# Count pieces of the second gathering layer moved ahead of its gathers, and two scatter tables filled from a small buffer, in a five-part graph network on one core

## The chip, the cores and the metric

The kernel runs on one core of one Trainium2 chip. The metric is device time of one execution in microseconds (us), lower is better. The kernel before was timed three times. The profile is of one execution more.

## The reference

Four graph layers follow one another on 6,250 nodes with 128 features, each ending in a residual sum and a layer norm. All share one list of 106,250 edges, sorted by target node.

```python
x = _layernorm(x + L0(x))   # segment_sum(weight * (x @ K)[dst], src) + bias
x = _layernorm(x + L1(x))   # sum over 8 bases b of segment_sum(alpha_b[type64] * (x[src] @ bases[b]), dst)
x = _layernorm(x + L2(x))   # relu(segment_sum(x[src] @ (W_data if type2 == 0 else W_control).T + b, dst) + x @ W_self.T + b_self)
x = _layernorm(x + L3(x))   # two graph convolutions with W1 and W2, normed by the degrees
```

Float32 results are kept by splitting a float32 table into three bf16 parts where a bf16 product is used.

## The kernel before, in words

The edges form 416 groups of 256, and 16 groups form a part (26 parts, each some 240 target nodes wide). The program is five passes, written out by hand for each engine as its own instruction stream. TensorE is `pe`, VectorE `dve`, ScalarE `act`, GpSimd `pool`, and `sp` only issues DMAs.

**Pass 0** (L0) is a scatter. In each of 52 bodies, four steps `k` make 4 tiles of 128 messages each. GpSimd adds them with indirect DMAs (L903) into four tables in device memory, `sums0` to `sums3`, in the fixed order 0, 1, 2, 3. A scatter into table `t` waits for the one before it into `t`. `sums0` starts as a copy of `x` (L883), `sums1` as the bias, written from a 2 KB buffer per partition (L884), `sums2` and `sums3` as zeros, written from the zeroed `acc`, 26 KB per partition (L892). The first zero fill waits until the product table `hx` is stored, the second until the first rows of `hx` are back (`xwin_in[0]`). `acc` is the upper part of `node_data`, where ScalarE also collects the adjacency counts of pass 0. So ScalarE waits for both fills before its first step. In the same pass TensorE counts edges per (source, target) pair (`build_adjacency`), ScalarE copies the counts to SBUF as integers (L1010) and stores them to `adj`.

**Pass 1** (L1) gathers rows of `t1` with indirect DMAs (L863, two per group, into a ring of 8 groups), multiplies them with weighted one-hots (`group_products`, L1325 and L1328), and once per part applies the eight bases (`base_piece`, L1416). Behind it run the stage steps of blocks of 256 nodes: TURN, RESIDUAL, NORM, TURN_ROWS, PROJECT (L1398, L1401), TABLE, then HI, REST, MID, LOW, which split the new rows into three bf16 parts and store them to `xp1` (L1150). The new table `t2` is stored by `sp` (L741, L744). There are 25 blocks (`NH`). The last two run after the last group, by themselves.

**Pass 2** (L2) covers the 26 parts in 13 pairs. Of each pair one part is gathered (32 indirect DMAs, L863, products at L1350), the other is computed from counts: seven pieces, each of 7 x 3 x 2 = 42 bf16 matmuls (`typed_piece`, L1506). A piece needs seven blocks of `x_parts`, the bf16 parts read back from `xp1` (L796), and two planes that ScalarE makes of a raw piece of counts (`to_planes`, L1166 and L1167, raw pieces loaded at L784). `typed_products` sets the order: two groups, one piece, and so on for eight steps, so that pieces stand in steps 0 to 6. Planes lie in `alpha`, the edge weights of pass 1. `x_parts` lies where pass 1 keeps its sums `G` and the last blocks' buffers.

**Passes 3 and 4** (L3) work alike with one plane per piece (L1447).

At the change from pass 1 to pass 2, `sp` waits until all of `xp1` and `t2` is stored and then loads all seven pieces of `x_parts`. TensorE waits for all seven before its first piece. ScalarE makes the first planes only when the last blocks are done. GpSimd starts gathering once `t2` is stored (`stored[1]`) and the first indices are copied (`idx_ready[2]`).

Of the kernel before, what the change touches and what calls it, by code (L numbers as in the profile page):

```python
# [41 lines left out]
P = 128  # L42
N = 6250
# [69 lines left out]
SET_FREE = (-3, 0, -1, 1, 2, 3, 5)  # L113
RAW2_USES = [RAW2.count(r) for r in range(3)]
# [42 lines left out]
def gnn_program(nc, src, src_row, dst, type2, type64, weight, x, xT0, k0, bias0, bases, rel_weights,  # L157
# [4 lines left out]
    with ctx:  # L162
# [351 lines left out]
        def sums_whole(eng, p, b):  # L514

            if p == 1:
                eng.wait_ge(based_added, NPT + 1 if isinstance(b, int) else b + (LAG + 1))
# [89 lines left out]
        def halves_in_steps(eng, stage_step, between=None):  # L607

            with eng.Fori(0, NH - 2) as b:
                if between:  # L610
                    between(b)
                for at in range(STEPS):
                    stage_step(b, 0, at)
            for at in range(STEPS):
                stage_step(NH - 2, 0, at)
                stage_step(NH - 1, 1, at)

# [8 lines left out]
        def parts_past(e):  # L626

            return {1: 0, 2: NH, 3: 2 * NH}[e]

# [42 lines left out]
        def _(sp):  # L672
# [91 lines left out]
            def reload_parts(layer, q):  # L764
# [7 lines left out]
                if q == NPC - 1:  # L772
                    sp.wait_ge(xp_in[NPC - 2], layer * 32 + 16)
# [3 lines left out]
            def load_typed(j, q):  # L777
                if q < 2:
                    sp.wait_ge(planes_ready, j * NPC + (q + 5))
                elif q < NPC - 1:  # L780
                    sp.wait_ge(planes_ready, j * NPC + (NPC + q - 1))
                else:
                    sp.wait_ge(planes_ready, j * NPC + NPC)
                sp.dma_start(raw2_in_words[RAW2[q]], adj[bass.ds(j * (2 * P) + 2 * P, P),  # L784
                                                         q * PIECE_H * CHUNK_COLS:(q + 1) * PIECE_H * CHUNK_COLS]
                             ).then_inc(raw_in[RAW2[q]], 16)
# [1608 lines left out]
```

## Time and profile before

| what | us |
|---|---|
| median of 3 runs | 4168.32 |
| lowest, highest | 4164.4, 4175.53 |
| the profiled execution | 4157.03 |
| its span, first to last instruction | 4155.0 |
| busy TensorE / GpSimd in the span | 3352.7 / 3052.5 |

The span is cut into slices and stretches. A row of the timeline has the start, the length, the engine, the line and what it does, and in brackets the engine's idle time just before and what ended it ("issue" is a wait for which the profile shows no releaser). Engine names with a q (SPq, ACTq) are DMA issues, whose data moves later. Busy TensorE is work issued, not array time.

### The profile page before, as it was taken

The page shows a single profiled execution, that of the slowest core. Times are in us where ns is not written, and L with a number is a line of the kernel's source. Part 1 is how long each engine was busy: PE and PEld are TensorE (multiplying, and loading weights), DVE is VectorE, ACT ScalarE, POOL GpSimd, SP SyncE. Part 2 cuts the span into 40 slices and gives each one's busy share as a digit, 9 for nine tenths or more (in the row PEclk, how much of TensorE's full clock was granted, in tenths as well). Part 3 has the DMA queues.
Part 4 walks back from the last instruction along what each step waited for, and adds up shares of the span by engine and source line. Part 5 has one row for each costly group of instructions (what it writes and reads, how often), then busy time and mean ns, then how long its engine had stood idle before and what let it go on. Part 6 is the DMA issues. An engine that isn't in the chain of part 4 may idle for free. (4 is left out here: it accounts for less than half of the span.)

```text
span 4155.0 us, 91543 instructions
## 1 busy us (share of the span) xinstructions
PE 3352.7 (81%) x22862; PEld 2502.8 (60%) x22863; DVE 2210.6 (53%) x6852; ACT 1988.2 (48%) x2741; POOL 3052.5 (73%) x2630
## 2 busy tenths in 40 slices
PE   3777777777777776178888878878999999999998
PEld 2444444444444444155565555557888888998887
DVE  6877777887878786545555555550222221211222
ACT  2666666666666665301111111115666666666664
POOL 1888888888888888677777777756666636774776
PEclk7888888888888787566766667668999999999999
DMA  8666666666666666612222222215444457778775
GB/s 272 118 127 116 117 119 126 114 117 128 117 117 119 125 115 135 218 53 61 65 63 63 65 61 65 61 56 176 129 141 136 133 199 225 232 224 269 224 232 163
DMA packets 348397, 560.71 MB, mean 135 GB/s; under 512 B 61692, under 2 KB 218532, under 8 KB 347396
## 3 DMA queue, kind: packets, MB, share of 16 engines
q0 software_dynamic: 177344, 183.67, 24.9%
q1 hardware_dynamic: 114710, 260.28, 20.0%
q10 hardware_dynamic: 56046, 113.91, 7.3%
q14 instruction: 246, 2.02, 0.2%
q8 instruction: 51, 0.84, 0.1%
HBM read 365.75 MB, written 195.26 MB: 135 GB/s over the span
## 5 line engine op out<-in xcount | busy, mean ns | idle before, releaser
L863 POOL DMA_INDIRECT rows<-t,idx_ring x1760 | 1685.1, 957 | 727.3 <-issue 602.9
L1597 PE MATMUL bank<-arena 128*128 128x384 bf16 (+1 forms) x2496 | 667.5, 396 | 394.2 <-DVE arena L2277 239.7
L1010 ACT ACTIVATE node_data<-bank,most_sb 128x384 f32 (+1 forms) x1248 | 671.6, 604 | 302.8 <-PE bank L1600 278.9
L903 POOL DMA_INDIRECT sums<-rows,idx_ring x416 | 663.4, 1595 | 146.8 <-issue 128.6
L903 POOL DMA_INDIRECT sums<-stage,idx_ring x416 | 661.3, 1590 | 126.8 <-issue 104.0
L1447 PE MATMUL bank<-alpha,arena 128*128 128x264 bf16 x5292 | 636.0, 276 | 0.0
L1447 PEld LDWEIGHTS bank<-alpha,arena 128*128 128x128 bf16 x5292 | 520.1, 101 | 72.9
L1328 PE MATMUL bank<-S,rows 128*128 128x192 f32 x1664 | 563.6, 481 | 0.0
L1597 PEld LDWEIGHTS bank<-arena 128*128 128x128 bf16 x2496 | 168.3, 106 | 601.1 <-issue 320.6
L1506 PE MATMUL bank<-alpha,arena 128*128 128x264 bf16 x3822 | 446.0, 276 | 16.0 <-ACT alpha L1167 9.3
L2276 DVE TENSOR_SCALAR arena<-S 128x1176 bf16<-128x1176 int16 x832 | 455.5, 547 | 1.9 <-issue 1.9
L1506 PEld LDWEIGHTS bank<-alpha,arena 128*128 128x128 bf16 x3822 | 374.2, 100 | 71.5 <-ACT alpha L1167 10.5
L1328 PEld LDWEIGHTS bank<-S,rows 128*128 128x128 f32 x1664 | 388.2, 270 | 15.5
L1325 PE MATMUL bank<-S01b,wgt 128*2 128x24 bf16 x832 | 112.9, 176 | 274.4 <-DMA rows<-t,idx_ring 227.5
L1325 PEld LDWEIGHTS bank<-S01b,wgt 128*2 (+1 forms) x832 | 54.3, 80 | 453.8 <-issue 336.1
L1576 PE MATMUL bank<-shared,wS 128*24 128x128 f32 x1664 | 268.0, 315 | 25.3 <-DVE wS L2249 25.1
L1350 PEld LDWEIGHTS bank<-S,rows 128*128 128x128 f32 x1856 | 234.7, 192 | 31.4 <-issue 27.7
L1350 PE MATMUL bank<-S,rows 128*128 128x24 f32 x1856 | 234.8, 256 | 23.1 <-DMA rows<-t,idx_ring 21.6
L1802 DVE TENSOR_TENSOR S<-iota_w,rel 128x96 f32<-128x96 f32 x232 | 59.0, 256 | 358.1 <-PE bank L1350 356.6
L1813 DVE TENSOR_TENSOR arena<-arena,bank 2x24 f32 x416 | 68.8, 165 | 338.6 <-PE bank L1328 332.7
L1600 PE MATMUL bank<-arena 128*128 128x16 bf16 (+1 forms) x1248 | 247.8, 199 | 0.0
L1586 PE MATMUL bank<-rows,arena 24*128 24x128 f32 x1664 | 244.4, 286 | 0.0
(227 smaller groups left out, 4617.9 us busy)
## 6 DMA issues: line engine op xcount, KB each, us to landing
shared<-adj SPq DMA_DIRECT2D x206, 462.0 KB
adj<-node_data ACTq DMA_DIRECT2D x189, 462.0 KB
S<-adj SPq DMA_DIRECT2D x62, 462.0 KB
arena<-adj SPq DMA_DIRECT2D x62, 462.0 KB
rows<-t,idx_ring POOLq DMA_INDIRECT x1760
arena<-src SPq DMA_DIRECT2D x104, 256.0 KB
arena<-xp SPq DMA_DIRECT2D x21, 672.0 KB, 6.9
arena<-type SPq DMA_DIRECT2D x52, 256.0 KB
```

What stands on the lines that cost most here:

```text
L863: nc.gpsimd.indirect_dma_start(out=rows[:, k, t, :], out_offset=None, in_=tables[p], in_offset=bass.IndirectOffsetOnAxis(ap=idx_ring[:, j, ...
L903: nc.gpsimd.indirect_dma_start(out=sums_t[t], out_offset=bass.IndirectOffsetOnAxis(ap=idx4[:, k, t:t + 1], axis=0), in_=msg[k][:, t, :], i ...
L1010: nc.scalar.activation(places[n][:, ha:hb, 0:W], bank[bk][:, 0:(hb - ha) * W].rearrange("p (h w) -> p h w", w=W), ACT.Identity, bias=most_ ...
L1328: last = nc.tensor.matmul(sums_bank(k)[:, 0:NB * W], rows[:, k, t, :], of_pair[:, t, :], start=t == 0, stop=t == GT - 1)
L1350: last = nc.tensor.matmul(bank[n % 2][:, bass.ds(at, W)], rows[:, k % RING, t, :], S2[:, slot, k % PAIR * GT + t, :], start=False, stop=k ...
L1447: last = nc.tensor.matmul(bank[to][:, 0:CHUNK_COLS], x_parts[:, q * PIECE_H + hh, part, :], adj_slot[n % NPC][:, hh * CHUNK_COLS:(hh + 1) ...
L1506: last = nc.tensor.matmul(bank[5 + 2 * t][:, 0:CHUNK_COLS], x_parts[:, q * PIECE_H + hh, part, :], planes[SETS[q]][t][:, at], start=q + hh ...
L1576: last = nc.tensor.matmul(bank[0][0:W, t * P:(t + 1) * P], wS[:, k % 2, t, :], sel[k % 2][:, t, :], start=True, stop=True)
L1586: last = nc.tensor.matmul(bank[4 + k % 2][:, t * P:(t + 1) * P], C[k % 2][:, t * P:(t + 1) * P], xwin[k][t // GT], start=True, stop=True)
L1597: nc.tensor.matmul(bank[bk][:, 0:(hb - ha) * W], lo, hw_hot[n * GT + t][:, ha * W:hb * W], start=t == 0, stop=False)
L1600: nc.tensor.matmul(bank[bk][:, 0:(hb - ha) * W:W], lo_last[before], hi_carry[before][:, ha:hb], start=False, stop=True).then_inc(ab_built, 1)
L2276: nc.vector.tensor_scalar(hw_hot[n * GT + t], iota_hw, hwi[:, e], None, ALU.is_equal)
```

## The change

What it does in pass 0: VectorE clears `stage[0]`, the 2 KB buffer of messages of step 2, before it clears `acc`. The two zero fills read `stage[0]`, 13 times per partition. The first now waits for the first load of source rows (`src_rows_in[0]`) in place of the store of `hx`. ScalarE no longer waits for the fills before its first step, only where it first writes `stage[0]`, at step 2.

What it does between passes 1 and 2: the pieces of pair 0 are computed in the order 0, 1, 2, 5, 3, 4, 6 (`FIRST_ORDER`), the first four of them (`IN_TAIL`) right behind the last blocks' projections and ahead of the first gathered group. `sp` loads the first two raw pieces before its loop of `t2` stores, pieces 0, 1, 2 of `x_parts` once the last `base_piece` is done, 5 after the last sum, and the other three as before. ScalarE makes planes 0 and 1 behind TURN_ROWS of block `NH - 3`, stores the last two blocks of `t2` itself, makes planes 2 between HI and MID and planes 3 after LOW of the last two blocks.

```diff
+FIRST_ORDER = (0, 1, 2, 5, 3, 4, 6)
+IN_TAIL = 4
...
-            with sp.Fori(0, NH - 1) as b:
-                sp.wait_ge(rows_ready[1], b + 2)
-                sp.dma_start(half_rows(t2_pairs, b), hst[1][0][:, 0:HALF * 2 * P].rearrange(
-                    "p (c f) -> p c f", c=HALF)).then_inc(stored[1], 16)
-            sp.wait_ge(rows_ready[1], NH + 1)
-            sp.dma_start(t2_pairs[(NH - 1) * HC:N, :], hst[1][1][0:LAST, 0:2 * P]).then_inc(stored[1], 16)
...
             sp.wait_ge(adj_stored, 16 * NPC * (NCHUNK + 1))
-            for q in range(2):
-                load_typed(0, q)
-            sp.wait_ge(xp_stored[1], 16 * (NH + 1))
+            for n in range(2):
+                load_typed(0, n)
+            with sp.Fori(0, NH - 2) as b:
+                sp.wait_ge(rows_ready[1], b + 2)
+                sp.dma_start(half_rows(t2_pairs, b), hst[1][0][:, 0:HALF * 2 * P].rearrange(
+                    "p (c f) -> p c f", c=HALF)).then_inc(stored[1], 16)
+            sp.wait_ge(xp_stored[1], 16 * (NH - 1))
+            sp.wait_ge(based, NPT)
+            for n in range(3):
+                load_typed_parts(FIRST_ORDER[n])
+            sp.wait_ge(based_added, NPT + 1)
+            load_typed_parts(FIRST_ORDER[3])
+            for n in range(2, 4):
+                load_typed(0, n)
             sp.wait_ge(stored[1], 16 * (NH + 1))
             sp.wait_ge(acc_set[1], NH + 1)
-            sp.wait_ge(based_added, NPT + 1)
-            for q in range(NPC):
-                sp.dma_start(x_parts[:, q * PIECE_H:(q + 1) * PIECE_H, :, :].rearrange("p h n f -> p (h n f)"),
-                             xp_d[1][:, q * PIECE_H * NPART * P:(q + 1) * PIECE_H * NPART * P]).then_inc(x2_in, 16)
-            sp.wait_ge(s_ready[1], NBODY * PAIRS + 1)
-            for q in range(2, NPC):
-                load_typed(0, q)
+            sp.wait_ge(xp_stored[1], 16 * (NH + 1))
+            for n in range(IN_TAIL, NPC):
+                load_typed_parts(FIRST_ORDER[n])
+            for n in range(4, NPC):
+                load_typed(0, n)
...
                 if t == 2:
-                    pool.wait_ge(hx_stored, 16 * (len(HXB) - 1))
+                    pool.wait_ge(src_rows_in[0], 16)
                 else:
                     pool.wait_ge(xwin_in[0], 16 * FHALF)
-                pool.dma_start(sums_t[t].rearrange("(p r) f -> p (r f)", p=P), acc[:, 0:TABR]).then_inc(scattered[t], 16)
+                pool.dma_start(sums_t[t].rearrange("(p b r) f -> p b (r f)", p=P, r=BLK),
+                               stage[0][:, :].unsqueeze(1).to_broadcast([P, NBLK, BC])).then_inc(scattered[t], 16)
...
                 act.wait_ge(scatter_through, i * FSTEPS + (k + 1))
+                if k == 2:
+                    for t in range(2, NTAB):
+                        act.wait_ge(scattered[t], 16)
...
-            for t in range(2, NTAB):
-                act.wait_ge(scattered[t], 16)
+            act.wait_ge(flag_ready, 1)
...
+            def planes_behind(b, at):
+
+                if b == NH - 3 and at == TURN_ROWS:
+                    act.wait_ge(s_ready[1], NBODY * PAIRS + 1)
+                    to_planes(0, 0)
+                    to_planes(0, 1)
+                elif b == NH - 1 and at == PROJECT:
+                    act.wait_ge(rows_ready[1], NH)
+                    act.dma_start(half_rows(t2_pairs, NH - 2), hst[1][0][:, 0:HALF * 2 * P].rearrange(
+                        "p (c f) -> p c f", c=HALF)).then_inc(stored[1], 16)
+                    act.wait_ge(rows_ready[1], NH + 1)
+                    act.dma_start(t2_pairs[(NH - 1) * HC:N, :], hst[1][1][0:LAST, 0:2 * P]).then_inc(stored[1], 16)
+                elif b == NH - 1 and at == HI:
+                    to_planes(0, 2)
+                elif b == NH - 1 and at == LOW:
+                    to_planes(0, 3)
...
-                    if at < NPC:
+                    if first and at < NPC - IN_TAIL:
+                        typed_piece(j, at + IN_TAIL, first)
+                    elif not first and at < NPC:
                         typed_piece(j, at, first)
...
                     stage_step(p, NH - 1, 1, at)
+                for n in range(IN_TAIL):
+                    typed_piece(0, n, True)
...
             dve.wait_ge(src_in, 16)
+            nc.vector.memset(stage[0][:, :], 0.0).then_inc(acc_zeroed, 1)
             nc.vector.memset(acc[:, :], 0.0).then_inc(acc_zeroed, 1)
```

On ScalarE, from PROJECT of the last two blocks on (L1080 sets `acc`, L1130 is HI, L1134 MID, L1150 the store of parts, L1166 and L1167 a pair of planes), there stood before:

```order
L1080 ACTIVATE node_data<-bank,bs_sb 128x256
L1080 ACTIVATE node_data<-bank,bs_sb 128x128
L1130 ACTIVATE arena<-arena 128x2x128
L1130 ACTIVATE arena<-arena 128x128
L1134 ACTIVATE arena<-arena 128x2x128
L1134 ACTIVATE arena<-arena 128x128
L1150 DMA xp<-arena 128x768
L1150 DMA xp<-arena 128x384
L1158 ACTIVATE dis<-dis,ones 128x49
L1166 ACTIVATE alpha<-shared 128x1848
L1167 ACTIVATE alpha<-shared,most_sb 128x1848
```

and now, with new line numbers (L1101, L1151, L1155 and L1171 for the four, L1180 and L1181 for planes, L1192 and L1195 for the stores of `t2`):

```order
L1101 ACTIVATE node_data<-bank,bs_sb 128x256
L1101 ACTIVATE node_data<-bank,bs_sb 128x128
L1192 DMA t<-arena 128x2x256
L1195 DMA t<-arena 106x256
L1151 ACTIVATE arena<-arena 128x2x128
L1151 ACTIVATE arena<-arena 128x128
L1180 ACTIVATE alpha<-shared 128x1848
L1181 ACTIVATE alpha<-shared,most_sb 128x1848
L1155 ACTIVATE arena<-arena 128x2x128
L1155 ACTIVATE arena<-arena 128x128
L1171 DMA xp<-arena 128x768
L1171 DMA xp<-arena 128x384
```

Two DMA issues stand ahead of HI, and one pair of planes between HI and MID.

On `sp` at the change from pass 1 to pass 2 (L741 and L744 store `t2`, L784 loads raw counts, L796 loads `x_parts`), there stood before:

```order
L741 DMA t<-arena 128x2x256
L739 REGISTER_ALU
L739 COMPARE_AND_BRANCH
L744 DMA t<-arena 106x256
L784 DMA shared<-adj 128x1848 x2
L796 DMA arena<-xp 128x2688 x7
L784 DMA shared<-adj 128x1848 x4
```

and now:

```order
L802 DMA t<-arena 128x2x256
L800 REGISTER_ALU
L800 COMPARE_AND_BRANCH
L794 DMA arena<-xp 128x2688 x4
L787 DMA shared<-adj 128x1848 x2
L794 DMA arena<-xp 128x2688 x3
L787 DMA shared<-adj 128x1848 x2
```

Four of the seven loads of `x_parts` and the third and fourth raw piece stand ahead of the last three loads, and the store of the last block is gone from this queue.

## Rows read from the trace of the kernel before

**Rows 1.** The page's 40 slices of the span, TensorE and GpSimd.

```profile
PE   3777777777777776178888878878999999999998
...
POOL 1888888888888888677777777756666636774776
```

**Rows 2.** Line L903, half the scatters: duration ns min/median/max, first and last start.

```profile
L903 POOL DMA_INDIRECT sums<-stage,idx_ring x416: 1551/1555/1847, 107.2 to 1668.2; - x139
```

**Rows 3.** Timeline of GpSimd, 0 to 130 us.

```profile
58.03 0.56 POOL L892 DMA_DIRECT2D sums<-node_data  x1 [30.99 <-DMA hx<-alpha]
70.88 0.53 POOL L892 DMA_DIRECT2D sums<-node_data  x1 [12.30 <-DMA rows<-hx]
91.80 1.67 POOL L903 DMA_INDIRECT sums<-rows,idx_ring  x1 [20.38 <-issue]
...
97.51 1.56 POOL L903 DMA_INDIRECT sums<-rows,idx_ring  x1 [0.30 <-issue]
```

**Rows 4.** Timelines of sp, VectorE and ScalarE, 0 to 130 us.

```profile
58.84 0.44 SPq L712 DMA_DIRECT2D arena<-src  x1
...
70.38 0.18 DVE L2238 COPY bank<-arena 128x16 f32 x1 [11.80 <-DMA arena<-src]
...
81.96 2.25 ACT L1023 ACTIVATE node_data<-zeros,most_sb 128x2352 f32 x1 [49.23 <-issue]
...
102.14 0.60 ACT L988 ACTIVATE stage<-bank 128x512 f32<-128x512 f32 x1 [0.79 <-PE bank L1586]
```

**Rows 5.** Stretches: length, busy PE, PEld, DVE, ACT, POOL, PEclk, DMA share, GB/s.

```profile
72.00:74.00 2.00, 1.56 (x8) 0.84 (x6) 1.50 (x6) 0.00 (x0) 0.00 (x0) 0.50 0.98 413
...
80.00:82.00 2.00, 0.00 (x0) 0.00 (x0) 1.44 (x5) 0.04 (x1) 0.00 (x0) 0.50 0.03 6
```

**Rows 6.** DMA queues of the page, and of the stretch 71 to 82: packets, MB, share.

```profile
q0 software_dynamic: 177344, 183.67, 24.9%
...
q0 software_dynamic: 144, 3.41, 72.6%
```

**Rows 7.** Timeline of GpSimd, 2700 to 2830 us.

```profile
2776.79 0.95 POOL L863 DMA_INDIRECT rows<-t,idx_ring  x1 [0.30 <-issue]
2809.37 0.95 POOL L863 DMA_INDIRECT rows<-t,idx_ring  x1 [31.63 <-issue]
```

**Rows 8.** Timeline of TensorE, 2768 to 2880 us.

```profile
2780.69 0.31 PE L1325 MATMUL bank<-S01b,wgt 128*2 128x24 bf16 x2 [1.71 <-DMA rows<-t,idx_ring]
...
2784.93 4.12 PE L1416 MATMUL bank<-arena,bases_sb 128*128 x16
...
2801.91 0.50 PE L1401 MATMUL bank<-arena,ws_sb 128*128 128x128 f32 x2
...
2826.75 6.18 PE L1506 MATMUL bank<-alpha,arena 128*128 128x264 bf16 x42 [6.64 <-DMA arena<-xp]
...
2833.58 4.88 PE L1506 MATMUL bank<-alpha,arena 128*128 128x264 bf16 x42
...
2868.10 0.97 PE L1350 MATMUL bank<-S,rows 128*128 128x24 f32 x8
```

**Rows 9.** Timelines of ScalarE, VectorE and sp about the change of passes.

```profile
2785.26 0.47 ACT L1080 ACTIVATE node_data<-bank,bs_sb 128x256 f32 x1 [7.73 <-PE bank L1401]
...
2804.99 0.17 DVE L1669 COPY idx_ring<-src_i 128x16 int32<-128x16 int32 x1
...
2802.60 0.28 SPq L744 DMA_DIRECT2D t<-arena  x1
```

**Rows 10.** Planes and the last S of pass 1: ScalarE from 2800 us, VectorE from 2768 us.

```profile
2809.08 1.74 ACT L1166 ACTIVATE alpha<-shared 128x1848 bf16<-128x1848 uint8 x1 [2.88 <-DMA shared<-adj]
2810.73 1.82 ACT L1167 ACTIVATE alpha<-shared,most_sb 128x1848 bf16<-128x1848 uint8 x1
...
2777.33 0.96 DVE L1792 TENSOR_TENSOR S<-bank,alpha 128x768 f32<-128x768 f32 x1
```

**Rows 11.** The stretch 2815 to 2826 us, with the columns of rows 5.

```profile
2815.00:2826.00 11.00, 2.09 (x8) 1.86 (x8) 0.26 (x1) 0.91 (x1) 8.26 (x10) 0.50 1.02 411
```

More of the change, by code:

```diff
@@ L516, in sums_whole @@
             if p == 1:
-                eng.wait_ge(based_added, NPT + 1 if isinstance(b, int) else b + (LAG + 1))
+                eng.wait_ge(based_added, NPT + 1 if isinstance(b, int) and b > NH - 3 else b + (LAG + 1))
             else:
@@ L605, in turned_count, with halves_in_steps @@
             return j * SLOTS + (NPC + layer * LPIECES + n + 1)
[L607 to L611, printed above, removed]
+        def halves_in_steps(eng, stage_step, between, behind):
+            with eng.Fori(0, NH - 3) as b:
+                between(b)
                 for at in range(STEPS):
                     stage_step(b, 0, at)
+            between(NH - 3)
+            for at in range(STEPS):
+                stage_step(NH - 3, 0, at)
+                behind(NH - 3, at)
             for at in range(STEPS):
@@ L616, in halves_in_steps @@
                 stage_step(NH - 1, 1, at)
+                behind(NH - 1, at)
         def past(e):
@@ L628, in parts_past, with typed_at @@
             return {1: 0, 2: NH, 3: 2 * NH}[e]
+        def typed_at(j, n):
+            return FIRST_ORDER[n] if isinstance(j, int) and j == 0 else n
         def sums_bank(k):
@@ L789, in _, with load_typed_parts @@
[L789 to L791 removed]
+                             ).then_inc(raw_in[RAW2[n]], 16)
+            def load_typed_parts(q):
+                if q == NPC - 1:
+                    sp.wait_ge(xp_in[NPC - 2], 16)
+                sp.dma_start(x_parts[:, q * PIECE_H:(q + 1) * PIECE_H, :, :].rearrange("p h n f -> p (h n f)"),
+                             xp_d[1][:, q * PIECE_H * NPART * P:(q + 1) * PIECE_H * NPART * P]).then_inc(xp_in[min(q, NPC - 2)], 16)
@@ L1151, in stage_step, with to_planes @@
                                   part_stage[e][k][:, 0:n, :, :].rearrange("p c n f -> p (c n f)")).then_inc(xp_stored[e], 16)
+            def to_planes(j, n):
+                r = RAW2[n]
+                act.wait_ge(raw_in[r], j * (16 * RAW2_USES[r]) + 16 * (RAW2[0:n].count(r) + 1))
+                act.wait_ge(dense_pieces, j * NPC + (NPC + SET_FREE[n]))
+                apart(act)
+                nc.scalar.activation(planes[SETS[n]][0], raw2[r][:, :, 0], ACT.Copy)
+                nc.scalar.activation(planes[SETS[n]][1], raw2[r][:, :, 1], ACT.Identity, scale=-1.0,
+                                     bias=most_sb[:, 0:1]).then_inc(planes_ready, 1)
@@ L1192, in typed_step @@
                     stage_step(2, a, 0, TURN, (j + ADDED_AHEAD, j))
-                to_planes(j, 1)
                 if stages:
+                    to_planes(j, 1)
                     stage_step(2, a, 0, NORM)
-                to_planes(j, 2)
-                to_planes(j, 3)
+                    to_planes(j, 2)
+                    to_planes(j, 3)
+                elif j > 0:
+                    for n in range(1, IN_TAIL):
+                        to_planes(j, n)
                 if stages:
@@ L1493, in summed_products, with typed_piece @@
                     last_blocks(4, stage_step)
-            def typed_piece(j, q, first):
-                pe.wait_ge(planes_ready, j * NPC + (NPC + q + 1))
-                if q == 0:
+            def typed_piece(j, n, first):
+                q = typed_at(j, n)
+                pe.wait_ge(planes_ready, j * NPC + (NPC + n + 1))
+                if n == 0:
                     pe.wait_ge(h_kept, j + 1)
-                if first and q == 0:
-                    pe.wait_ge(x2_in, 16 * (2 + NPC))
+                if first and n == 0:
+                    pe.wait_ge(based_added, NPT + 1)
+                if first:
+                    pe.wait_ge(xp_in[min(q, NPC - 2)], 32 if q == NPC - 1 else 16)
                 for hh in range(PIECE_H):
@@ L1506, in typed_piece @@
                             last = nc.tensor.matmul(bank[5 + 2 * t][:, 0:CHUNK_COLS], x_parts[:, q * PIECE_H + hh, part, :],
-                                                    planes[SETS[q]][t][:, at], start=q + hh + part == 0,
-                                                    stop=q == NPC - 1 and hh == PIECE_H - 1 and part == NPART - 1)
+                                                    planes[SETS[n]][t][:, at], start=n + hh + part == 0,
+                                                    stop=n == NPC - 1 and hh == PIECE_H - 1 and part == NPART - 1)
                 last.then_inc(dense_pieces, 1)
```

34 lines of the change are left out of this document (12 added, 22 removed).

## The prediction

> **What bounds the kernel now.** I read the slices of the span first, then for each of the two places that the diff touches the timelines of the engines that meet there.
>
> The slices [rows 1] show TensorE at 9 tenths only in the last third; in the first sixteen GpSimd holds 8 tenths. The scatters say why. The first starts at 91.80 [rows 3], the last at 1668.2 [rows 2], and there are 832 of them: 1576.4 / 831 = 1.897 us from start to start, against a median of 1.555 us for one and the 0.30 us that stands before each [rows 2, 3]. So GpSimd issues without a break, and pass 0 lasts from its first scatters as long as 832 issues take. A start moved by 1 us moves the end of pass 0, and all behind it, by 1 us.
>
> Before that start there is a hole. VectorE waits 11.80 us for the source rows, issued at 58.84, and ScalarE stands 49.23 us until both zero fills have landed, to 81.96 [rows 4]. The first fill was issued at 58.03, just ahead of the source rows, the second at 70.88 [rows 3].
>
> At the change from pass 1 to pass 2 GpSimd is idle 31.63 us, from its last gather at 2776.79 to 2809.37 [rows 7], and TensorE ends its last projection at 2802.4 and starts its first piece at 2826.75, released by the load of `x_parts` [rows 8]. From there to the end TensorE is full.
>
> A measurement of this kernel can tell about 0.3% from no change, here 12.5 us.
>
> **The start of pass 0.** Removed: the wait of ScalarE for both fills; the first fill's place ahead of the source rows. Added: 0.4 us of clearing `stage[0]` on VectorE, beside loads that end at 58, so hidden (if it weren't, it would cost 0.4).
>
> Source rows. Without a fill ahead of them, the type rows and source rows are two loads of 256 KB. At the 413 GB/s that the engines reach when full [rows 5] that is 1.3 us, and a landing takes some 1.9 us more (data at 6 GB/s from 80, ScalarE released at 81.96 [rows 4, 5]). From 58.84 they land near 62.5, not 70.38. VectorE starts its first step 7.9 us earlier.
>
> Fills. The first is issued at 62.5, the second when `xwin_in[0]` is full. Its loads go out at once, behind at most one fill's data, so the second is queued before the first is done, and the two follow each other without a gap. A fill is 3.41 MB [rows 6]. Two of them, one more load of source rows (0.26 MB), two stores of counts that ScalarE now makes in this time (0.95 MB) and small ones are 8.0 MB, or 19.4 us at 413 GB/s. With 0.9 us before the first data and 1.9 for the landing: 62.5 + 0.9 + 19.4 + 1.9 = 84.7; I take 85.
>
> Who waits now. The scatters 0, 1 and 2 need messages of step 0, which come some 16 us earlier than before and so near 74. The fourth, into `sums3`, needs the second fill, 85. Before it started at 97.51 [rows 3]. From 85 on GpSimd again issues without a break: ScalarE's write of step 2, the one that waits for the fills, lay 20.2 us behind its own start (81.96 to 102.14 [rows 4]) and its scatters follow the fourth by another four issues, 7.6 us. **Gain 97.5 - 85 = 12.5 us.** Bounds: if the source rows land no earlier than now, the fills end at 70.4 + 22.2 = 92.6 and 5 us are left; if the counts' stores stay behind the fills, 2.3 us more, 15.
>
> The fills' source is a new shape for them: 2 KB pieces read 13 times in place of 26 KB rows. Nearest rows: 413 GB/s for the long rows, and 183.67 MB in 24.9% of the 16 engines' span (4155.0 us), 178 GB/s, for the whole software queue, most of it scatters and gathers of 512-byte rows [rows 5, 6]. The second is a floor far away, since the pieces are four times as long. I take the first, and keep the other for a rival.
>
> The Trainium skill, DMA: Bandwidth & Descriptors, in "Anatomy of one DMA", gives a DMA of GpSimd as 2.0 us and the bytes over 436 GB/s. That estimate makes a fill 9.8 us where this trace shows 11.1 from issue at 70.88 to the release at 81.96; by it the fills would end near 83 and the gain be 14 to 15. The row decides here.
>
> **The change of passes.** Moved: four pieces, to where TensorE waits. What each of them needs:
>
> Planes 0 and 1. The last S, which reads `alpha`, ends at 2778.3 [rows 10]. A pair of planes takes 3.5 us (2809.08 to 2812.55 [rows 10]), two pairs end at 2785.3. ScalarE would have been idle 7.73 us, to 2785.26 [rows 9]. So they fit to within 0.1 us.
>
> `x_parts` 0, 1, 2 and 5. `base_piece` ends at 2789.1 [rows 8]. Loads go out near 2791: 4 x 0.69 MB and then two raw pieces of 0.47 MB are 3.7 MB, 9.0 us at 413 GB/s, with the landing 2802. TensorE comes at 2802.4. Pieces 0 to 3 then run to 2802.5 + 6.2 + 3 x 4.9 = 2823.4, the first at the low clock as now (6.18 against 4.88 [rows 8]); planes 2 (2804 to 2807.6) and 3 (from 2810) are ready in time.
>
> Queued behind. Two DMA issues of 0.35 us now stand ahead of HI on ScalarE, and planes 2 ahead of MID. MID, REST's successor LOW on VectorE, and the copy of indices follow some 4.2 us later: `idx_ring` at 2809.2 and not 2804.99 [rows 9]. GpSimd waits for that and for the store of the last block. The last was issued by sp at 2802.60 [rows 9], and is now issued by ScalarE at 2803.3, as the second of two. GpSimd started at 2809.37 with indices long there, so the store decided; 0.7 us on it gives 2810.1, after the indices. Cost 0.7, up to 4 if the indices come late.
>
> What is bound now. With four pieces gone, the eight steps of pair 0 hold 3 x 5.5 us and are limited by gathers. One step takes two groups, four gathers. A part has 32 gathers, and its first piece stands behind its second group, so the 36th gather of pass 2 decides when the second gathered part gets going: 2810.1 + 35 x 1.257 (the spacing of pass 1's gathers, 0.95 and 0.30 [rows 7]) = 2854.1, and with 0.95 and the 2.95 us from the end of a gather to its products (2777.74 to 2780.69 [rows 7, 8]) that group runs at 2858.0. Now the first two groups of this part run at 2868.10 [rows 8]: 10.1 us. So of some 21 us of pieces moved, half is given back to gathers. GpSimd may not stall on its ring of eight meanwhile: the seventh group must be done before its 15th wants the slot, near 2845.4; with planes 4 at 2825 and steps of 5.5 us it is done at 2842. Slack 3 us.
>
> Clock. In 2815 to 2826 TensorE was busy 2.09 of 11 us at a granted clock of 0.50, the 1.2 GHz level [rows 11]. In the new steps 3 to 7 it is busy 0.8 of 5 us, so I expect the low level when part 1 starts. That costs what the first piece costs now, 6.18 - 4.88 = 1.3 us, and 0.3 on its groups. **Gain 10.1 - 1.6 = 8.5 us.** Bounds: 12, if the store lands sooner without two loads of counts beside it and the clock holds; 2, if the indices come 4 us late and ScalarE's planes cost the rest.
>
> After part 1 a step is 5.5 us of TensorE (34.5 us for six and the projection, 2833.58 to 2868.10 [rows 8]) against 5.0 of gathers, so the lead stays. The passes behind shift as a whole.
>
> **Sum.** 12.5 + 8.5 = 21 us. The profiled execution would go from 4157.03 to 4136.0. It lies 11.3 us under the median of the runs shown; on that median 4168.32 - 21 = 4147.3.
>
> **The rivals.**
>
> A, *gathers keep the second gain* (15%): the pieces fill the hole, but planes, `x_parts` or indices come late, GpSimd stalls on its ring, and part 1 starts near 2866. For it: the slack is 3 us and three conditions meet there. Against: each was worked out with its own row. With 10 to 12 us from the start the sum is 11, 4157.
>
> B, *both gains at their upper bounds* (10%): the source rows and fills as fast as a quiet queue allows, 15 + 12 = 27 us, 4141.
>
> C, *one gain only, the start* falls to its lower bound (7%): the source rows were late for a reason other than the fill ahead of them. 5 + 7 = 12 us, 4156.
>
> D, *slower* (3%): the fills from 2 KB pieces. Were they to run F us each, the fourth scatter starts at 62.5 + 2 F + 5.7 (0.9 ahead, 1.9 landing, 2.9 for the other 1.2 MB). The start loses from F = 14.7 on, and the whole is slower from F = 18.9, or 180 GB/s, about the floor above. Slower by more than 0.3% needs 25.2 us each, 135 GB/s. At 22 us each it is 6 us slower, 4174. Against it speaks that the bias went out of such a buffer before.
>
> E, the change does nothing at the start because something other than GpSimd bounds pass 0: the spacing of 1.897 us excludes it.
>
> **How the numbers follow.** The forecast holds the remaining 65%, its own range 4141 to 4153. With A, B and C, and some 4 us by which medians of a few runs differ (they spread from 4164.4 to 4175.53), 4135 to 4160 holds 8 in 10. Faster by over 0.3% is a gain of over 12.5 us: forecast, B, and parts of A and C, 0.82. Within 0.3%: 0.15. Slower: 0.03.
>
> **What would show it.** In the new profile: first source rows at 62 to 63; the fourth scatter at 83 to 87, and 1.90 us between scatters after; the first gather of pass 2 at 2809 to 2811 less the first gain; four pieces in a row right behind the last projection, the first one slow; the second gathered part right behind the 36th gather. Wrong would be a fourth scatter after 92, a gap ahead of the four pieces, or GpSimd waiting for TensorE inside pair 0.

## The result, and the profile after

| us | kernel before | changed kernel |
|---|---|---|
| median of 10 runs each | 4167.76 | 4153.33 |
| lowest, highest | 4159.92, 4187.36 | 4148.86, 4158.6 |
| the profiled execution | 4157.03 | 4153.56 |
| its span | 4155.0 | 4151.5 |

The ratio is 0.9958, with a 95% interval of 0.9946 to 0.9970: 17.5 us faster (12.5 to 22.5). The medians are 14.4 us apart. Forecast were 4147.3 us and a gain of 21. The direction was right, and 4153.33 lies in the wide range (4135 to 4160) and just outside the forecast's own (4141 to 4153); a gain of 21 is near the upper end of what the interval allows, and more than the medians show. The two profiled executions are only 3.5 us apart, so it takes more than these two to see where the gain is.

The page's slices of the changed kernel, TensorE, GpSimd and the granted clock:

```profile
PE   4777778777777786177888878779999999999998
...
POOL 2888888888888888677777777757766637774775
PEclk7888877788778877566767666669999999999999
```

They look as before [rows 1]; the change is small against a slice of 104 us. The start of pass 0 on GpSimd, VectorE and ScalarE (start, length, engine, line; idle time before and what ended it in brackets):

```profile
62.58 2.23 POOL L910 DMA_DIRECT2D sums<-stage  x2 [36.13 <-DMA arena<-src]
76.28 1.71 POOL L922 DMA_INDIRECT sums<-rows,idx_ring  x1 [11.46 <-issue]
87.68 1.56 POOL L922 DMA_INDIRECT sums<-rows,idx_ring  x1 [5.95 <-DVE idx_ring L2310]
...
62.44 0.18 DVE L2285 COPY bank<-arena 128x16 f32 x1 [2.91 <-DMA arena<-src]
...
94.34 0.60 ACT L1010 ACTIVATE stage<-bank 128x512 f32<-128x512 f32 x1 [1.73 <-PE bank L1632]
```

The source rows are there at 62.4 and not 70.38 [rows 4], both fills go out in a row, and the fourth scatter starts at 87.68 in place of 97.51 [rows 3]. It waited for the second fill: the copy of indices named in its row stands behind a count that GpSimd gives only once that fill has landed. All scatters, by line: duration in ns min/median/max, first and last start:

```profile
L922 POOL DMA_INDIRECT sums<-rows,idx_ring x416: 1556/1561/1986, 76.3 to 1651.5; - x139
L922 POOL DMA_INDIRECT sums<-stage,idx_ring x416: 1555/1561/1871, 97.2 to 1667.3; - x139
```

Against [rows 2] the last one starts at 1667.3 and not 1668.2. Of 9.8 us at the start, 0.9 are left, since one scatter follows the other in 1.908 us and not 1.897. Of these 11 ns, 6 are in the median scatter (1561 ns and not 1555); most of the rest is in the longer ones, as the mean is 1602 ns and not 1592, and the idle time before one is 0.31 us in both.

The change of passes on GpSimd, ScalarE, VectorE and TensorE:

```profile
2775.97 0.95 POOL L881 DMA_INDIRECT rows<-t,idx_ring  x1 [0.30 <-issue]
2808.80 0.95 POOL L881 DMA_INDIRECT rows<-t,idx_ring  x1 [31.87 <-DVE idx_ring L1715]
...
2784.36 0.45 ACT L1101 ACTIVATE node_data<-bank,bs_sb 128x256 f32<-128x256 f32 x1
...
2807.40 0.17 DVE L1715 COPY idx_ring<-src_i 128x16 int32<-128x16 int32 x1
...
2800.96 19.06 PE L1548 MATMUL bank<-alpha,arena 128*128 128x264 bf16 x168
2823.35 6.57 PE L1548 MATMUL bank<-alpha,arena 128*128 128x264 bf16 x42 [2.41 <-ACT alpha L1181]
...
2848.98 1.04 PE L1389 MATMUL bank<-S,rows 128*128 128x24 f32 x4 [2.48 <-DMA rows<-t,idx_ring]
...
2856.25 7.68 PE L1548 MATMUL bank<-alpha,arena 128*128 128x264 bf16 x42
...
2864.58 4.88 PE L1548 MATMUL bank<-alpha,arena 128*128 128x264 bf16 x42
```

The row of 168 matmuls is four pieces, and they follow the last projection without a gap. From 2845 on TensorE waits for gathers, as the waits in brackets say, and the second gathered part runs right behind its rows. Its second piece starts 88.6 us behind the last gather of pass 1; before, at 2874.44, it was 97.65 (2776.79 [rows 7]).

### The profile page after: what moved, and what is told of

The parts are those of the page before. It is cut to its first block and busy times, and to the rows that moved or that the text cites. A ratio compares the mean times of both kernels' runs of the same rounds, so it can differ in the third digit from the quotient of the medians.

```text
span 4151.5 us, 91583 instructions
## 1 busy us (share of the span) xinstructions
PE 3402.2 (82%) x22862; PEld 2529.4 (61%) x22863; DVE 2210.4 (53%) x6853; ACT 1991.8 (48%) x2741; POOL 3062.1 (74%) x2630
## 5 line engine op out<-in xcount | busy, mean ns | idle before, releaser
L1643 PE MATMUL bank<-arena 128*128 128x384 bf16 (+1 forms) x2496 | 690.3, 407 | 359.3 <-DVE arena L2324 225.0
L1632 PE MATMUL bank<-rows,arena 24*128 24x128 f32 x1664 | 255.2, 295 | 0.0
```

The costliest lines, as they stand in the source:

```text
L1632: last = nc.tensor.matmul(bank[4 + k % 2][:, t * P:(t + 1) * P], C[k % 2][:, t * P:(t + 1) * P], xwin[k][t // GT], start=True, stop=True)
L1643: nc.tensor.matmul(bank[bk][:, 0:(hb - ha) * W], lo, hw_hot[n * GT + t][:, ha * W:hb * W], start=t == 0, stop=False)
```

## The experiments

Executions of one kernel differ, and the chips differ too, so each ratio below is against the kernel before on the same chip, and the mechanisms are read from positions in the traces. "Last scatter" and the like are times from the start of the span. Spacing is (last - fourth scatter) / 828.

### The two parts apart, and both kernels again

The first kernel has the fills' part of the diff alone, the second the pieces' part alone; the other two are both kernels unchanged.

Expected of the fills alone:

> Only the part of the change at the start of pass 0. The pace of the scatters decides. Theory 1, the pace does not depend on the change and differs from execution to execution: fourth scatter near 87.7 in place of 97.5, spacing anywhere from 1.897 to 1.908 us, and against the kernel before 8 to 10 us faster (ratio 0.9976 to 0.9981). Theory 2, the change itself slows the scatters by 11 ns each: fourth scatter near 87.7, spacing 1.908, last scatter within 1.5 us of 1668.2, and the time within 2 us of the kernel before (ratio 0.9995 to 1.0005).

Expected of the pieces alone:

> Only the part of the change between passes 1 and 2. Both theories: fourth scatter near 97.5, the first piece of the second gathered part 9 to 10 us nearer to the last gather of pass 1 than before, 7 to 9 us faster (ratio 0.9979 to 0.9983). Theory 1: spacing of scatters anywhere from 1.897 to 1.908. Theory 2: spacing 1.897 as before, since the fills are as before.

Expected of the kernel before:

> The kernel before, one more execution, for its pace in pass 0. Theory 1 (the pace differs from execution to execution): spacing from the fourth scatter to the last off 1.897 by 5 ns or more. Theory 2 (the change slows the scatters): 1.897 again, within 2 ns.

Expected of the changed kernel:

> The changed kernel, one more execution. Theory 1: spacing of the scatters off 1.908 by 5 ns or more, or overlapping with that of the kernel before. Theory 2: 1.908 again, within 2 ns. Fourth scatter at 87 to 88 by both.

| | fourth scatter | last scatter | spacing | median scatter, ns | ratio |
|---|---|---|---|---|---|
| before, profile above | 97.51 | 1668.23 | 1.8970 | 1555 | |
| before again | 98.80 | 1671.48 | 1.8994 | 1555 | |
| pieces alone | 98.90 | 1671.25 | 1.8990 | 1555 | 0.9984 (0.9972 to 0.9996) |
| changed, profile above | 87.68 | 1667.31 | 1.9078 | 1561 | 0.9958 (0.9946 to 0.9970) |
| changed again | 90.56 | 1665.25 | 1.9018 | 1560 | |
| fills alone | 90.02 | 1664.96 | 1.9021 | 1560 | 0.9992 (0.9981 to 1.0003) |

Neither theory holds whole. The pace does differ between executions of one kernel (1.9078 and 1.9018), but by the duration of a single scatter the kernels fall into two groups: 1555 ns without the new fills, 1560 or 1561 with them. The start is won (9 us), and then more than half of it is lost again. The spacings separate less well. Over all executions with none of the new fills (four, with one below) they are 1.8970 to 1.9000, over all with two of them (nine, with six below) 1.9001 to 1.9078; the averages, 1.8989 and 1.9036, differ by 4.8 ns, or 4.0 us in 828 scatters.

By the ratios the fills alone gave 3.3 us (-1.3 to 7.9) and the pieces alone 6.7 (1.7 to 11.7), 10 together against 17.5 for both in one kernel. The intervals are wide enough to hold a plain sum, so no extra gain from having both is shown. The profile of the fills alone was of the longest of its 12 executions, 4176.17 us, and shows one thing that sets executions apart. In pass 3 TensorE waited twice:

```profile
3578.47 4.45 PE L1450 MATMUL bank<-alpha,arena 128*128 128x264 bf16 x21 [6.25 <-ACT alpha L1189]
3672.44 4.80 PE L1450 MATMUL bank<-alpha,arena 128*128 128x264 bf16 x21 [6.43 <-ACT alpha L1189]
```

Each costs the wait of some 6.3 us and some 2 us for the piece behind it, which ran at a granted clock of 0.55 and 0.50 and takes 2.53 us otherwise. Of thirteen executions (all but the one on a slower chip, below), four had waits of 6 us for planes, two of them twice: this one, the one with two pieces ahead, and once each the ones with fills from ScalarE and with the split store. The rest had none. Before and changed kernel, twice each, are among the rest. What decides about them stays open.

### Where the scatters' 5 ns come from

Fills from long rows, at their new place, ScalarE waiting for both:

```diff
-                pool.dma_start(sums_t[t].rearrange("(p b r) f -> p b (r f)", p=P, r=BLK),
-                               stage[0][:, :].unsqueeze(1).to_broadcast([P, NBLK, BC])).then_inc(scattered[t], 16)
+                pool.dma_start(sums_t[t].rearrange("(p r) f -> p (r f)", p=P), acc[:, 0:TABR]).then_inc(scattered[t], 16)
...
-            act.wait_ge(flag_ready, 1)
+            for t in range(2, NTAB):
+                act.wait_ge(scattered[t], 16)
```

> The changed kernel with the fills read from the 26 KB rows again, and ScalarE waiting for both before its first step, as in the kernel before; their place behind the source rows stays. Theory 1, the form of the fills (2 KB pieces) makes each later scatter 5 ns longer: scatters of 1.555 us again, spacing 1.897 to 1.900. Theory 2, something else of the change makes them longer (the place of the fills, the program around the loop): 1.560 or 1.561 us. By both, the fills end near 84 to 86, the first step of ScalarE starts then, and the fourth scatter comes near 100 to 103; ratio 0.9975 to 0.9990.

```profile
L921 POOL DMA_INDIRECT sums<-rows,idx_ring x416: 1551/1555/1947, 94.3 to 1657.8; - x139
```

1555 ns again, as theory 1 had it, with spacing 1.9000, fourth scatter at 100.30 and ratio 0.9977 (0.9965 to 0.9989). Next, one fill of each form, with the same wait:

```diff
-                pool.dma_start(sums_t[t].rearrange("(p b r) f -> p b (r f)", p=P, r=BLK),
-                               stage[0][:, :].unsqueeze(1).to_broadcast([P, NBLK, BC])).then_inc(scattered[t], 16)
+                if t == 2:
+                    pool.dma_start(sums_t[t].rearrange("(p b r) f -> p b (r f)", p=P, r=BLK),
+                                   stage[0][:, :].unsqueeze(1).to_broadcast([P, NBLK, BC])).then_inc(scattered[t], 16)
+                else:
+                    pool.dma_start(sums_t[t].rearrange("(p r) f -> p (r f)", p=P), acc[:, 0:TABR]).then_inc(scattered[t], 16)
```

> The changed kernel with one fill in 2 KB pieces and the other from 26 KB rows, ScalarE waiting for both before its first step. Theory 1, each such fill adds its share to every later scatter: median scatter 1.557 to 1.558 us. Theory 2, a step at some point: 1.555 or 1.560 us. The fourth scatter near 100 by both; the time says little (4155 to 4165).

```profile
L925 POOL DMA_INDIRECT sums<-rows,idx_ring x416: 1552/1556/1846, 95.5 to 1659.3; - x139
```

Shortest and median scatter, 1552 and 1556 ns, are each 1 ns above those with fills from rows, and 4 below those of the run with both fills in pieces and this wait (1556 and 1560, below). The two executions of the changed kernel differ by 1 ns as well (1561 and 1560). So one new fill, into `sums2`, costs 1 ns or nothing, and not half of 5; the new form for `sums3` alone was not run. Then both fills through ScalarE's queue:

```diff
-                if t == 2:
-                    pool.wait_ge(src_rows_in[0], 16)
-                else:
-                    pool.wait_ge(xwin_in[0], 16 * FHALF)
-                pool.dma_start(sums_t[t].rearrange("(p b r) f -> p b (r f)", p=P, r=BLK),
-                               stage[0][:, :].unsqueeze(1).to_broadcast([P, NBLK, BC])).then_inc(scattered[t], 16)
+                pool.dma_start(sums_t[t][0:1, :], stage[0][0:1, 0:P]).then_inc(scattered[t], 16)
+            pool.wait_ge(hx_stored, 16 * (len(HXB) + 1))
...
                 if k == 2:
-                    for t in range(2, NTAB):
-                        act.wait_ge(scattered[t], 16)
+                    act.wait_ge(hx_stored, 16 * (len(HXB) + 1))
...
             act.wait_ge(flag_ready, 1)
+            for t in range(2, NTAB):
+                act.wait_ge(scattered[t], 16)
+            act.wait_ge(hx_stored, 16 * (len(HXB) - 1))
+            for t in range(2, NTAB):
+                act.dma_start(sums_t[t].rearrange("(p b r) f -> p b (r f)", p=P, r=BLK),
+                              stage[0][:, :].unsqueeze(1).to_broadcast([P, NBLK, BC])).then_inc(hx_stored, 16)
```

> The changed kernel with both fills issued by ScalarE, through its hardware queue, near 58; through GpSimd's queue goes one row of each table, and GpSimd waits for both fills before its first scatter. Theory 1, 2 KB fills that pass GpSimd's own queue make each later scatter 5 ns longer: here scatters of 1.555 us, spacing 1.897 to 1.900, first scatter near 83, last near 1660. Theory 2, what counts is that the tables were filled in 2 KB pieces, by whatever queue: 1.560 us, last near 1664. Ratio to the kernel before 0.9935 to 0.9950.

```profile
L918 POOL DMA_INDIRECT sums<-rows,idx_ring x416: 1557/1562/1932, 80.7 to 1651.1; - x139
```

1562 ns: taking the big fills out of GpSimd's queue gives nothing back (one row of each table still passes it). The first scatter came at 80.7 and not near 83, the last at 1666.05 and not 1664, and the ratio is 0.9960 (0.9945 to 0.9975), above the 0.9935 to 0.9950 expected. Last, the wait of ScalarE alone:

```diff
-            act.wait_ge(flag_ready, 1)
+            for t in range(2, NTAB):
+                act.wait_ge(scattered[t], 16)
```

> The changed kernel with the wait of ScalarE for both fills put back ahead of its first step; both fills stay in 2 KB pieces and at their new place. The run with fills from 26 KB rows differed from the changed kernel in two things, the rows and this wait, and this run has the wait alone. Theory 1, the form of the fills makes the scatters longer: 1.560 or 1.561 us, at most 2 of 832 at 1.55 or less. Theory 2, the early start of ScalarE does it: 1.555 to 1.556 us, over 200 at 1.55 or less. By both the fills end near 87, ScalarE starts then, the fourth scatter comes near 102, and the ratio to the kernel before is 0.997 to 0.999.

```profile
L922 POOL DMA_INDIRECT sums<-rows,idx_ring x416: 1556/1560/1848, 95.2 to 1661.4; - x139
```

1560 ns and none of 832 at 1.55 us or less (449 to 472 of them in the four executions with no new fill), so it is not ScalarE's early start: with the same wait, fills from 26 KB rows leave scatters of 1555 ns and fills from 2 KB pieces 1560. The two runs were on different chips, but on each of two other chips both lengths were seen, 1555 and 1560. So the form of the fills is shown to be the cause, where form means two things that were never parted: pieces of 2 KB in place of 26, and `stage[0]` in place of `acc` as the buffer that is read. By what path it reaches scatters a millisecond later is not shown: passing the large fills through GpSimd's queue is excluded, and where GpSimd's descriptors lie or how its program sits in memory were not tried.

This run fell on a chip on which passes 1 to 4 are slower (the kernel before took 4674.11 us there). Its ratio, 1.0029 (1.0015 to 1.0043), missed the 0.997 to 0.999 expected and is for that chip only. The changed kernel was not timed there, so whether the change wins anything on such a chip is not known. Pass 0 ran as on the others (fourth scatter 101.05, last 1676.30).

### Fills earlier

```diff
                 if t == 2:
-                    pool.wait_ge(src_rows_in[0], 16)
-                else:
-                    pool.wait_ge(xwin_in[0], 16 * FHALF)
+                    pool.wait_ge(hx_stored, 16 * (len(HXB) - 1))
```

> The changed kernel with both fills issued when the product table is stored, near 58, ahead of the source rows' load. Theory 1, pieces of the fills and of the source rows share the engines: source rows near 64, both fills landed near 81 to 83, fourth scatter at 82 to 84 in place of 87.7 to 90.6, 4 to 6 us faster than the changed kernel (ratio to the kernel before 0.9943 to 0.9950). Theory 2, a load issued behind a fill waits for the whole fill whatever its pieces: source rows near 76 to 78, fourth scatter after 95, 5 to 8 us slower than the changed kernel (0.9968 to 0.9978). By both, scatters of 1.561 us as in the changed kernel.

```profile
58.66 2.23 POOL L908 DMA_DIRECT2D sums<-stage  x2 [31.47 <-DMA hx<-alpha]
...
79.91 1.71 POOL L920 DMA_INDIRECT sums<-rows,idx_ring  x1 [19.01 <-issue]
...
85.69 1.56 POOL L920 DMA_INDIRECT sums<-rows,idx_ring  x1 [0.30 <-issue]
...
66.08 0.18 DVE L2283 COPY bank<-arena 128x16 f32 x1 [7.17 <-DMA arena<-src]
```

The source rows, now behind a fill of 2 KB pieces, land at 66.1. Behind a fill from 26 KB rows it was 70.38 [rows 4], and ahead of the fills 62.4. Its load was issued at 59.47, 0.8 us behind the fill in both kernels. So the short pieces let the load through, and theory 1 holds in kind, though the rows came 2 us and the fourth scatter 1.7 us after what it said. The rest of the hole is now set by messages: the scatters follow one another from 79.91 on. The last scatter is at 1661.66, 4.6 us before the changed kernel's two on average. Ratio 0.9946 (0.9931 to 0.9960), median 4144.52 against 4166.25, the lowest median of the runs; its interval overlaps the changed kernel's.

### Two pieces ahead in place of four

```diff
+PE_TAIL = 2
...
-                    if first and at < NPC - IN_TAIL:
-                        typed_piece(j, at + IN_TAIL, first)
+                    if first and at < NPC - PE_TAIL:
+                        typed_piece(j, at + PE_TAIL, first)
...
-                for n in range(IN_TAIL):
+                for n in range(PE_TAIL):
```

This is on TensorE alone; the orders of ScalarE and `sp` stay.

> The changed kernel with TensorE doing two pieces ahead of the gathered groups in place of four, five between them. Theory 1, the 36th gather decides when the second gathered part starts: first gather as before the edit, second part again right behind the 36th gather, so within 1 us of the changed kernel there, and up to 3 us better because TensorE is busier and its first pieces run at the high clock; ratio to the kernel before 0.9945 to 0.9958. Theory 2, TensorE's pieces decide: second part 9.8 us later, ratio 0.9980.

The view is TensorE's timeline. The two pieces, then the waits ahead of the first two groups, and the second piece of the second part:

```profile
2797.61 9.94 PE L1549 MATMUL bank<-alpha,arena 128*128 128x264 bf16 x84
...
2811.61 0.78 PE L1390 MATMUL bank<-S,rows 128*128 128x24 f32 x4 [3.95 <-DMA rows<-t,idx_ring]
2815.11 1.04 PE L1390 MATMUL bank<-S,rows 128*128 128x24 f32 x4 [2.71 <-DMA rows<-t,idx_ring]
...
2853.73 6.13 PE L1549 MATMUL bank<-alpha,arena 128*128 128x264 bf16 x42
...
2860.51 4.88 PE L1549 MATMUL bank<-alpha,arena 128*128 128x264 bf16 x42
```

2860.51 is 88.5 us behind the last gather of pass 1 (2771.97), as with four pieces (88.6 and 88.3). TensorE's share was not the bound; gathers are, and two of the four pieces moved win nothing. The first piece of the second part took 6.13 us in place of 7.68. That can't be laid to this edit, since with four pieces ahead it took anything from 6.14 us (fills earlier) over 6.55 (changed kernel again) to 7.68. Ratio 0.9953 (0.9938 to 0.9968), not to be told from the changed kernel's.

### Indices earlier

```diff
-                copy_idx(p, body, 0)
+                if p > 2:
+                    copy_idx(p, body, 0)
...
                     stage_step(p, NH - 1, 1, at)
+                    if at == TURN_ROWS:
+                        copy_idx(2, 0, 0)
```

> The changed kernel with the first indices of pass 2 copied on VectorE between NORM and TABLE of the last blocks, near 2799, in place of behind LOW, near 2807.4. Theory 1, indices and the store of the last block come within 0.3 us of each other, so nothing but 0 to 0.5 us of first gather is won; ratio 0.9955 to 0.9960. Theory 2, only the indices held the gathers: first gather 28 to 29 us behind the last one in place of 32.8, and the second gathered part 3.5 to 4.5 us earlier; ratio 0.9945 to 0.9950.

From the last gather to the first of pass 2 it took 32.11 us; in the eight other executions with the pieces moved, those with the split store and on the slow chip left out, 32.83 to 33.79. So indices cost about 1 us (0.7 to 1.7), more than theory 1's 0.5 and far from theory 2's 4, and what is then last is the store of the last block. Ratio 0.9951 (0.9936 to 0.9967), too wide to choose between the two. The stretch in which GpSimd waits for that store (length, busy TensorE, its clock, DMA share, GB/s):

```profile
2799.30:2803.50 4.20, 4.20 (x40) 1.00 0.12 34
```

A DMA share of 0.12 is 2 of 16 engines. The Trainium skill, DMA: Bandwidth & Descriptors, in "Why a DMA increments its semaphore by 16 and not by 1", says that a DMA is served by the largest number of engines up to 16 that divides the outer sizes at both its ends. For 106 rows that is 2, and the row agrees.

### The last rows split, with the two edits above

```diff
+EVEN = 96
...
-                    act.dma_start(t2_pairs[(NH - 1) * HC:N, :], hst[1][1][0:LAST, 0:2 * P]).then_inc(stored[1], 16)
+                    act.dma_start(t2_pairs[(NH - 1) * HC:N - LAST + EVEN, :], hst[1][1][0:EVEN, 0:2 * P]).then_inc(stored[1], 16)
+                    act.dma_start(t2_pairs[N - LAST + EVEN:N, :], hst[1][1][EVEN:LAST, 0:2 * P]).then_inc(stored[1], 16)
```

The same goes for `t3` and `t4`; waits for the last store count one more.

> The changed kernel with early fills and early indices as in the two runs on these, and the last 106 rows of each of t2, t3 and t4 stored as 96 and 10 rows. Theory 1, the store of 106 rows moves at 12 to 47 GB/s because few DMA engines serve it, and 96 rows go to all: first gather of pass 2 2 to 3 us nearer to the last one of pass 1 (29.5 to 30.5 us in place of 32.1), TensorE's wait for first gathers of pass 3 (8.2 us) 2 us shorter, and of pass 4 as well; with 6 us from early fills and 2 from early indices, 12 us faster than the changed kernel, ratio 0.9925 to 0.9935. Theory 2, the store is slow for another reason (row length, latency): the first gather as in the run with early indices, ratio 0.9938 to 0.9948.

```profile
2774.06 0.95 POOL L882 DMA_INDIRECT rows<-t,idx_ring  x1 [0.30 <-issue]
2803.82 0.95 POOL L882 DMA_INDIRECT rows<-t,idx_ring  x1 [28.81 <-issue]
```

29.76 us in place of 32.11: theory 1 at the change to pass 2. At pass 3 TensorE waited 6.16 us for its first gathers and at pass 4 3.44 us, where the run with early indices had 6.04 and 2.93: no gain there, so the store doesn't seem to be last there. Ratio 0.9940 (0.9919 to 0.9962), where 0.9925 to 0.9935 was expected; median 4150.6 against 4168.3, with one wait of 6 us in pass 3 in the profiled execution. It beats the kernel before. The interval overlaps that of the changed kernel (0.9946 to 0.9970), so it isn't shown to beat that one, nor the run with the fills issued earlier alone.

## Why the prediction was right, and where not

**GpSimd bounds pass 0: right.** Behind the fourth scatter GpSimd hardly ever waits: over the 828 scatters its idle time before one is 0.305 to 0.307 us on average in each of the fourteen executions, against 0.30 as the usual step, and at most two of them had more than 0.6 us before them.

**The start, forecast 12.5 us: 9.0 at the fourth scatter, 3.6 at the last** (means of the two executions of each kernel: 98.2 to 89.1, and 1669.9 to 1666.3). The source rows came at 62.4 as worked out. Two steps failed, and both are terms of the sum that were too small. The first is the time of the two fills. From their issue to the scatter that waits for them it was forecast at 22.5 us and took 25.1 (62.58 to 87.68) and 26.4 (64.14 to 90.56). The forecast took 8.0 MB at 413 GB/s. The stretch from the issue to the last of the fills' data, with the columns of [rows 5], says otherwise:

```profile
62.58:86.16 23.58, 18.23 (x92) 10.71 (x93) 19.82 (x60) 9.79 (x17) 7.08 (x5) 0.57 0.96 366
```

The engines were full, but moved 366 GB/s, and 8.6 MB (8.9 in the second execution). Without ScalarE's work beside them the two fills took 22.05 us in pieces and 20.4 from rows, as ScalarE's first instruction shows in the run with its wait alone and in the one with fills from rows; they were issued at 62.97 and 62.83:

```profile
85.02 2.25 ACT L1045 ACTIVATE node_data<-zeros,most_sb 128x2352 f32 x1 [51.88 <-issue]
```

```profile
83.27 2.25 ACT L1044 ACTIVATE node_data<-zeros,most_sb 128x2352 f32 x1 [50.44 <-issue]
```

So the form costs the fills themselves about 1.6 us, and the rest of the excess is the traffic beside them. The second is the pace. "From 85 on GpSimd again issues without a break" was true, with another price for one issue. I bounded the new form by what the fills themselves cost, and held 1.897 us as fixed. Most of its cost lay in the 828 scatters behind them: 5 ns in each are 4.1 us, which is what all executions show on average (4.0), and the spacings of the two pairs of executions (1.8982 and 1.9048 on average) make 5.5 us.

**The change of passes, forecast 8.5 us: 9.5** (from the last gather to the second piece of the second part 97.65 and 98.29 us in the kernel before, 88.61 and 88.27 in the changed one). Planes 0 and 1 fitted (2784.36 for 2785.3 forecast), the four pieces met no gap, and the 36th gather decides, as the run with two pieces shows. It came 44.0 us behind the first (2808.80 to 2852.81), the forecast's 35 x 1.257. Three details were off. The first of the four ran at full pace and not at 6.2 us. The first gather was held by indices as well as by the store, at 32.83 and 33.54 us behind the last gather, against 32.58 and 32.74 before: 0.5 us later, and not for the store alone. And the low clock behind the gather-bound steps cost more than the forecast 1.3 us, 7.68 - 4.88 = 2.8, and 1.7 in the second execution (6.55). Here is the stretch about its start (length, busy TensorE, its clock, DMA share, GB/s):

```profile
2842.00:2853.00 11.00, 6.38 (x34) 0.63 0.46 137
```

GpSimd never stood on its ring ahead of that gather, as its pace of 1.257 us shows, so rival A fell.

**"The passes behind shift as a whole": nearly.** Pass 2 added a little (first piece of pass 3 609.6 us behind the last gather of pass 1, before 619.7, means of two: 10.1 us). Passes 3 and 4 took 5.0 us longer: from that piece to the end of the span 758.9 and 762.0 us before, 765.8 and 765.0 after. That the change causes this is not shown, since the runs with fills earlier and with indices earlier, which hold all of the change behind pass 0, took 761.6 and 759.9. A part of it stands in the opening of pass 3. Of the kernel before, TensorE's first piece behind a wait of 3.2 us for VectorE, and the stretch around it:

```profile
3408.42 2.53 PE L1447 MATMUL bank<-alpha,arena 128*128 128x264 bf16 x21
```

```profile
3375.00:3440.00 65.00, 60.43 (x530) 1.00 0.71 244
```

and of the changed kernel, behind a wait of 3.1 us:

```profile
3397.85 4.19 PE L1486 MATMUL bank<-alpha,arena 128*128 128x264 bf16 x21
```

```profile
3375.00:3440.00 65.00, 52.36 (x441) 0.94 0.83 286
```

The granted clock fell behind almost the same wait. It fell so in neither execution of the kernel before and in both of the changed one, but also in that with the fills alone, in which this place is untouched (4.83 us), and not at this piece with the fills issued early (clock 0.95 over the stretch) or with two pieces ahead, where it took 2.53 us. Whether the change causes it stays open.

**The sum.** By positions 9.0 at the start less 5.4 for the pace, 0.8 by the last gather of pass 1, 10.1 for the change of passes and less 5.0 for passes 3 and 4 make 9.5 us, which is what the spans of the two pairs show (4159.1 to 4149.6). The medians show 14.4 and the ratio 17.5. Two executions of each kernel are too few to close that gap, and the first profile of the kernel before, 4157.03 us, is quicker than all ten of its timed runs (4159.92 and up). What the usual run of it holds in addition was not seen, so 5 to 8 us of the measured gain have no place in this account.

The terms that forecast 21 were 12.5 and 8.5; the first was too large, by the fills' end and above all by the scatters' pace, the second about right. By positions the two made 3.6 and 9.5, 13 us, next to the 12 of rival C, which had another reason for a small gain at the start. That the time still fell into the range is in part the range's width, and in part gain that the positions don't show: for the first term it was luck. Rival D, a price of the 2 KB pieces, had the right object and the wrong place: the fills ran nearly as well as from rows, and the price came later and small.

## What to carry to other kernels

A start moved ahead of a loop bound by one engine is worth its microseconds only if each turn of that loop costs the same after: multiply a few ns by the number of turns before banking it, and read the median of one instruction at the loop's end as well as the time of its first. When work fills a hole, ask how much of it the next bound gives back; here two pieces did what four did. And a short load behind a long one was delayed less here where the long one came in short pieces.

## What was not expected of the hardware

- Two zero fills from 2 KB pieces of a small buffer, in place of 26 KB rows, left the median scatter of GpSimd at 1560 to 1562 ns and not 1555, for 1.6 ms, also when they went through ScalarE's queue. One such fill left 1556.
- A store of 106 rows kept 2 of 16 DMA engines busy, at 34 GB/s; as 96 and 10 rows it let the gathers start 2.4 us earlier.
- Source rows behind a fill landed at 66.1 with 2 KB pieces and at 70.4 with 26 KB rows, for the same bytes.
- One chip took 4674 us for the kernel before, where the others took 4166 to 4168; in the one profile from it, pass 0 ran as elsewhere (last scatter at 1676.30), and passes 1 to 4 were slower.
